# Adding gathered node rows to edge rows inside the indirect transfer of a graph network's edge stage

## The chip, the cores and the metric

The kernel is one program on 1 core of one Trainium2 chip. The metric is the device time of one launch in microseconds (us). Three runs of the kernel before gave 6792.09, 6813.02 and 6817.62 us; the median, 6813.02 us, is "the time before".

## The reference, cut to what matters

The network has four layers on 6250 nodes with 256 features each: a graph convolution, a routed feed-forward layer, a message-passing layer over 106250 edges, and a second routed feed-forward layer. The change touches only the third one. All arithmetic is in float32.

```python
def mish(x):
    return x * jnp.tanh(jax.nn.softplus(x))
x = mish(node_features @ W_dense.T + b_dense)      # one row of 256 per node
y = mish(edge_features @ W_edge.T + b_edge)        # one row of 256 per edge
msg = jax.nn.relu(x[src] + y)                      # gather a node row for each edge, add, relu
agg = jax.ops.segment_sum(msg, dst, num_segments=node_features.shape[0])
rst = x + agg
return mish(rst @ W_out.T + b_out)
```

The edges are sorted by their destination `dst`; the sources `src` are random.

## The kernel before

The program is a row of stages with a barrier of all engines between them. Two of them matter here.

**The node stage, `stage_node_mish`.** It makes x for all nodes, 52 tiles of 128 nodes in 13 groups of 4, each group as two halves h. For a half, TensorE (PE) transposes the normalised rows (`ps_t`), ScalarE (ACT) evacuates them, PE multiplies with the dense weights into `ps_y`, VectorE (DVE) clips the product into `q`, ACT makes a factor out of `q` with four activations, and DVE's `finish` turns factor and product into the mish rows: L1259 forms 1 - q, L1261 multiplies it by `ps_y` into `rows`. Only after L1261 is `ps_y[h]` free (`py_free`) for PE's next product. SyncE (SP) stores `rows` to the DRAM table `node_table`, from which the edge stage gathers; PE transposes `rows` back into `ps_u`, and DVE's `keep` (L1269) copies that into the feature table in SBUF (`c.feat`, "messages_table" in the profile), where the sums over edges are added later.

**The edge stage, `stage_edges`.** An earlier stage has left the mish of every edge row in the DRAM table `edge_mish_table`, with the sign turned: it holds -y. The edge stage has 210 groups of 512 edges (4 columns of 128 edges each, one edge per partition), walked as 35 iterations i of 6 slots s. The steps for one group are:

- SP loads the 512 KB of -y into one of three buffers `neg` (L1397), when `neg_free` says that the buffer's last group is summed.
- GpSimd (POOL) issues 4 indirect transfers (L1410), one for each column of 128 edges, which fetch the node rows `x[src]` into one of six buffers `node`. The row numbers come from `idx`, which DVE fills for three slots at once (`indices`, L1457). POOL waits for them once per three slots; nothing else holds it.
- DVE makes the 0/1 matrices `hot` (which edge belongs to which of 64 destinations, L1441), waits for `neg` and for the 4 gathers, and subtracts: `node - neg` (L1446), which is x + y.
- ACT applies relu in place (L1435).
- PE sums by 16 matmuls of `node` with `hot` into `ps_a` (L1425).
- DVE adds `ps_a` to the feature table (`add`, L1454).

DVE's queue goes: hot and subtraction for slot s, then the `add` of slot s-1, with the `indices` of the second half behind the `add` of step 0 and those of the next iteration's first half behind the `add` of step 3. So the index copy that lets POOL begin three slots stands behind a subtraction, and that subtraction waits for a gather. Every queue is in order, and the order is the written one.

## Time and profile before

| | us |
|---|---|
| median of three runs (lowest, highest) | 6813.02 (6792.09, 6817.62) |
| span of the profiled execution | 6977.8 |
| node stage, about 4300 to 4495 in the span | 195 |
| edge stage, about 4495 to 5880 in the span | 1385 |

The profiled execution is one run with the hardware profiler on. The profile gives its span, from the first to the last instruction, and no further time around it; the span is 164.8 us above the median. In the whole span PE is busy for 59% of the time, POOL 42%, DVE 29% and ACT 22%. POOL's time is nearly all the issue of indirect transfers.

### The profile page before, as it was taken

To read this page: it belongs to the slowest core of one execution; us is meant where nothing else is said; L and a number is where in the kernel's file an instruction comes from. 1 tells how busy PE (TensorE), PEld (TensorE's weight loads), DVE (VectorE), ACT (ScalarE), POOL (GpSimd) and SP (SyncE) were. 2 spreads that over 40 slices of the span, in tenths; PEclk is the share of its full clock that TensorE was granted. 3 is DMA by queue.
4 is the path that set the end of the run, shared out by engine and by line. 5 is a ranking of instruction groups with operands and counts; after the bars stand their busy time and mean duration, and the time that the engine had idled before them with its cause. 6 is when DMAs were issued, how large, how long until landed. Compare 5 with 4: busy or idle time off the path is not lost. (4 is left out here: it accounts for less than half of the span.)

```text
span 6977.8 us, 63984 instructions
## 1 busy us (share of the span) xinstructions
PE 4133.3 (59%) x16404; PEld 3120.9 (45%) x16404; DVE 2046.0 (29%) x4123; ACT 1510.4 (22%) x1776; POOL 2925.0 (42%) x3015
## 2 busy tenths in 40 slices
PE   3676666676567666666532962655555555616990
PEld 2444444444344444434322851455555554415780
DVE  4223222222222222222441334332222323421212
ACT  1223222223223222222210101311111112301110
POOL 0555554453455554454114013166666664041005
PEclk8666666666666666666566985655555555558995
DMA  2344443343233333233203222254554553013213
GB/s 93 119 130 134 131 132 124 120 135 115 94 104 112 102 102 104 95 98 103 52 23 111 82 84 60 68 162 155 161 162 159 160 165 101 1 60 116 66 59 112
DMA packets 347713, 744.50 MB, mean 107 GB/s; under 512 B 68177, under 2 KB 196313, under 8 KB 347538
## 3 DMA queue, kind: packets, MB, share of 16 engines
q1 hardware_dynamic: 161522, 392.68, 16.4%
q0 software_dynamic: 118176, 284.72, 14.2%
q10 hardware_dynamic: 67968, 66.60, 3.0%
q14 instruction: 33, 0.27, 0.0%
q8 instruction: 14, 0.23, 0.0%
HBM read 521.40 MB, written 222.32 MB: 107 GB/s over the span
## 5 line engine op out<-in xcount | busy, mean ns | idle before, releaser
L565 PE MATMUL conv_pz<-conv_we,conv_edge 128*128 128x256 f32 x3360 | 1394.5, 536 | 505.5 <-issue 500.4
L446 POOL DMA_INDIRECT conv_gath<-support_table,conv_idx x840 | 811.8, 966 | 890.0 <-POOLq L55 631.2
L1410 POOL DMA_INDIRECT x_node<-node_table,x_idx x840 | 874.0, 1040 | 711.5 <-POOLq L55 460.1
L446 POOL DMA_INDIRECT conv_gath<-hidden_table,conv_idx x840 | 807.2, 961 | 868.3 <-POOLq L55 619.5
L565 PEld LDWEIGHTS conv_pz<-conv_we,conv_edge 128*128 128x128 f32 x3360 | 794.9, 258 | 795.9 <-issue 677.2
L1425 PE MATMUL x_pa<-x_hot,x_node 128*128 128x64 f32 x3360 | 755.4, 422 | 627.5 <-PEq L55 377.0
L1425 PEld LDWEIGHTS x_pa<-x_hot,x_node 128*128 128x128 f32 x3360 | 729.1, 331 | 654.1 <-issue 654.1
L556 PE MATMUL conv_ps<-conv_hot,conv_gath 128*128 128x64 f32 x3360 | 588.2, 331 | 497.4 <-issue 200.6
L556 PEld LDWEIGHTS conv_ps<-conv_hot,conv_gath 128*128 128x128 f32 x3360 | 538.3, 243 | 537.8 <-issue 412.1
L1206 ACT ACTIVATE conv_q<-conv_q 128x1024 f32<-128x1024 f32 x210 | 221.9, 1057 | 2218.0 <-ACTq L55 1919.6
L456 DVE TENSOR_SCALAR conv_q<-conv_pz 128x1024 f32<-128x1024 f32 x210 | 257.2, 1225 | 1463.2 <-DVEq L55 1214.2
L1435 ACT ACTIVATE x_node<-x_node 128x1024 f32<-128x1024 f32 x210 | 221.8, 1056 | 1160.4 <-ACTq L55 1011.4
L1007 POOL COPY cb_idx<-row 128x8 int32 x24 | 4.8, 200 | 846.0 <-POOLq L55 845.9
L1110 PE MATMUL e_ph<-e_xt,e_w_first 128*128 128x256 f32 x1376 | 318.9, 389 | 61.9 <-PEq L55 61.9
L566 PE MATMUL conv_pz<-conv_bias_parts,conv_ones 3*128 3x256 bf16 x840 | 273.4, 326 | 100.7 <-issue 99.3
L1145 ACT ACTIVATE e_hid<-e_ph,e_b_first 128x256 f32<-128x256 f32 x344 | 138.1, 474 | 856.7 <-ACTq L55 856.7
L472 DVE TENSOR_TENSOR sums_table<-sums_table,conv_ps 128x64 f32 x420 | 93.2, 222 | 772.4 <-DVEq L55 614.7
L1110 PEld LDWEIGHTS e_ph<-e_xt,e_w_first 128*128 128x128 f32 x1376 | 262.7, 194 | 108.6 <-issue 73.3
L566 PEld LDWEIGHTS conv_pz<-conv_bias_parts,conv_ones 3*128 3x128 bf16 x840 | 78.9, 94 | 500.2 <-issue 500.2
L1446 DVE TENSOR_TENSOR x_node<-x_node,x_neg 128x1024 f32<-128x1024 f32 x210 | 257.0, 1224 | 149.8 <-DMA x_node<-node_table,x_idx 129.9
L1454 DVE TENSOR_TENSOR messages_table<-messages_table,x_pa 128x128 f32 x210 | 60.1, 286 | 769.8 <-DVEq L55 632.2
L272 PE MATMUL e_pt<-ident_sb,e_rows 128*128 128x128 f32 x456 | 61.4, 278 | 354.0 <-PEq L55 354.0
(213 smaller groups left out, 4461.1 us busy)
## 6 DMA issues: line engine op xcount, KB each, us to landing
conv_edge<-in_edge_t SPq DMA_DIRECT2D x210, 512.0 KB
edge_mish_table<-conv_neg SPq DMA_DIRECT2D x210, 512.0 KB
x_neg<-edge_mish_table SPq DMA_DIRECT2D x210, 512.0 KB
e_rows<-expert_rows SPq DMA_DIRECT2D x114, 256.0 KB, 3.7
expert_outs<-e_outs ACTq DMA_DIRECT2D x114, 256.0 KB, 2.2
expert_rows<-conv_zeros ACTq DMA_DIRECT2D x35, 512.0 KB
expert_outs<-conv_zeros ACTq DMA_DIRECT2D x35, 512.0 KB
conv_gath<-support_table,conv_idx POOLq DMA_INDIRECT x840
```

The source lines that it names most:

```text
L446: pool.indirect_dma_start(gath[s][:, j, :], None, table[:, :], bass.IndirectOffsetOnAxis(ap=idx[:, half, col:col + 1], axis=0),).then_inc( ...
L456: nc.vector.tensor_scalar(q[r][:], ps_z[r][:], ZMAX, None, ALU.min).then_inc(z_ready[r], 1)
L556: last = pe.matmul(ps[s % 2][:], gath[s][:, j, :], hot[half][:, at + j, :], start=j == 0, stop=j == CG - 1)
L565: pe.matmul(ps_z[r][:, j, :], edge[r][:, m, j * P:(j + 1) * P], we[:, m, :], start=m == 0, stop=False)
L566: last = pe.matmul(ps_z[r][:, j, :], ones[:], parts[:], start=False, stop=True)
L1110: last = pe.matmul(out[:, m, :], w[:, k, m * P:(m + 1) * P], given[:, k, :], start=k == 0, stop=k == KD - 1)
L1145: last = act.activation(hid[h][:, m, :], ps_h[h][:, m, :], (ACT.Relu, ACT.Gelu)[mix], bias=b_first[:, e, m:m + 1])
L1206: link(act, act.activation(q, q, ACT.Exp), own)
L1410: pool.indirect_dma_start(node[s][:, j, :], None, c.t3[:, :], bass.IndirectOffsetOnAxis(ap=idx[:, half, col:col + 1], axis=0),).then_inc(g ...
L1425: last = pe.matmul(ps_a[n][:, m, :], node[s][:, j, m * P:(m + 1) * P], hot[n][:, j, :], start=j == 0, stop=j == CG - 1)
L1435: act.activation(node[s][:], node[s][:], ACT.Relu).then_inc(msg_ready, 1)
L1446: nc.vector.tensor_tensor(node[s][:], node[s][:], neg[s % RING][:], ALU.subtract).then_inc(own, 1)
```

## The change

It has three parts.

- The edge stage no longer has `neg` buffers. SP loads the -y rows into `node[s]` itself, six buffers instead of three, and the indirect transfers add the gathered rows onto them (`compute_op=ALU.add`). POOL therefore waits for SP's load (`neg_in[s]`) before the 4 transfers of every slot. SP waits for `node_free[s]`, which DVE signals when the slot's sum is ready.
- The subtraction L1446 is gone. ACT waits for the gathers itself and applies relu with scale -1. DVE's matrices get a semaphore of their own (`hot_ready`), for which PE waits beside `msg_ready`.
- For this, the gathered rows have to be -x. The node stage makes them in one instruction, (q - 1) * `ps_y`, in place of the two of `finish`; `keep` turns the sign back with a multiplication in place of the copy.

```diff
             def finish(h):
                 take(dve, q_ready[h])
-                link(dve, nc.vector.tensor_scalar(q[h][:], q[h][:], -1.0, 1.0, ALU.mult, ALU.add), own)
                 take(dve, rows_out[h], 16)
-                link(dve, nc.vector.tensor_tensor(rows[h][:], q[h][:], ps_y[h][:], ALU.mult), own)
+                link(dve, nc.vector.scalar_tensor_tensor(rows[h][:], q[h][:], -1.0, ps_y[h][:], ALU.add, ALU.mult), own)
...
-                nc.vector.tensor_copy(tokens(c.feat[:, :, :], g, h), ps_u[h][:])
+                nc.vector.tensor_scalar(tokens(c.feat[:, :, :], g, h), ps_u[h][:], -1.0, None, ALU.mult)
...
                     for s in range(SLOTS):
-                        take(sp, neg_free[s % RING])
-                        sp.dma_start(neg[s % RING][:], c.mish_d[...]).then_inc(neg_in[s % RING], 16)
+                        take(sp, node_free[s])
+                        sp.dma_start(node[s][:], c.mish_d[...]).then_inc(neg_in[s], 16)
...
                         take(pool, idx_ready[half])
                         for s in range(half * 3, half * 3 + 3):
+                            take(pool, neg_in[s], 16)
                             for j in range(CG):
                                 col = (s - half * 3) * CG + j
                                 pool.indirect_dma_start(
                                     node[s][:, j, :], None, c.t3[:, :],
                                     bass.IndirectOffsetOnAxis(ap=idx[:, half, col:col + 1], axis=0),
+                                    compute_op=ALU.add,
                                 ).then_inc(gathered[s], 16)
...
+                        take(pe, hot_ready)
                         take(pe, msg_ready)
...
-                        take(act, own)
-                        act.activation(node[s][:], node[s][:], ACT.Relu).then_inc(msg_ready, 1)
+                        act.wait_ge(gathered[s], k * (IT * CG * 16) + i * (CG * 16) + CG * 16)
+                        act.activation(node[s][:], node[s][:], ACT.Relu, scale=-1.0).then_inc(msg_ready, 1)
...
-                take(dve, neg_in[s % RING], 16)
-                dve.wait_ge(gathered[s], k * (IT * CG * 16) + i * (CG * 16) + CG * 16)
-                nc.vector.tensor_tensor(node[s][:], node[s][:], neg[s % RING][:], ALU.subtract).then_inc(own, 1)
...
                 take(dve, sum_ready)
-                dve.sem_inc(neg_free[s % RING], 1)
+                dve.sem_inc(node_free[s], 1)
```

DVE's queue at the start of the edge stage's steady loop, before, for slot 0 and half of slot 1 (x_hot are the 0/1 matrices, x_node the gathered rows, x_idx the row numbers for POOL):

```order
L1441 TENSOR_TENSOR x_hot<-iota_sb,x_rel 128x256
L1445 ISA
L1446 TENSOR_TENSOR x_node<-x_node,x_neg 128x1024
L1449 ISA
L1449 TENSOR_LOAD x_window
L1449 ISA x2
L1454 ISA
L1454 TENSOR_TENSOR messages_table<-messages_table,x_pa 128x2x64
L1457 ISA
L1457 COPY x_idx<-src_sb 128x12
```

The same place with the change:

```order
L1443 TENSOR_TENSOR x_hot<-iota_sb,x_rel 128x256
L1448 ISA
L1448 TENSOR_LOAD x_window
L1448 ISA x2
L1453 ISA
L1453 TENSOR_TENSOR messages_table<-messages_table,x_pa 128x2x64
L1456 ISA
L1456 COPY x_idx<-src_sb 128x12
```

The subtraction has left the queue. What stands behind it, the addition of the slot before and the index copy, now stands behind the 0/1 matrices alone.

POOL's loop over one iteration, before (a row names the semaphores for which the first of its transfers waits; the names are those of earlier stages that held the same semaphores, here the two `idx_ready`):

```order
L1410 DMA x_node<-node_table,x_idx 128x256 [waits s_rows_ready0]
L1410 DMA x_node<-node_table,x_idx 128x256 x11
L1410 DMA x_node<-node_table,x_idx 128x256 [waits s_rows_out1]
L1410 DMA x_node<-node_table,x_idx 128x256 x11
```

With the change, for the first half and the first slot of the second:

```order
L1410 DMA x_node<-node_table,x_idx 128x256 [waits s_py_ready1,s_rows_out1]
L1410 DMA x_node<-node_table,x_idx 128x256 x3
L1410 DMA x_node<-node_table,x_idx 128x256 [waits conv0_w_in]
L1410 DMA x_node<-node_table,x_idx 128x256 x3
L1410 DMA x_node<-node_table,x_idx 128x256 [waits conv0_edge_in1]
L1410 DMA x_node<-node_table,x_idx 128x256 x3
L1410 DMA x_node<-node_table,x_idx 128x256 [waits s_rows_ready0,conv0_edge_in2]
L1410 DMA x_node<-node_table,x_idx 128x256 x3
```

The 12 transfers of a half are cut into three times 4, each behind a wait for the slot's load; the wait for the indices has stayed where it was.

## Rows read from the trace of the kernel before

**Rows 1.** Windows of node and edge stage: busy us of each engine, clock, DMA share, GB/s.

```profile
4300.00:4495.00 195.00, 153.65 (x468) 91.41 (x468) 78.54 (x154) 80.73 (x131) 0.00 (x0) 0.64 0.10 35
4495.00:5880.00 1385.00, 755.41 (x3360) 729.06 (x3360) 403.26 (x706) 221.84 (x210) 874.71 (x841) 0.50 0.51 159
```

**Rows 2.** Groups by line, 4520 to 5860: busy us, mean ns, idle before, releasers.

```profile
L1410 POOL DMA_INDIRECT x_node<-node_table,x_idx x822 | 855.5, 1041 | 486.2 <-issue 245.9 <-POOLq L55 240.0 <-DVE x_idx L1457 0.3
L1425 PE MATMUL x_pa<-x_hot,x_node 128*128 128x64 f32 x3279 | 737.2, 422 | 603.3 <-PEq L55 354.3 <-issue 220.4 <-ACT x_node L1435 28.3
...
L1446 DVE TENSOR_TENSOR x_node<-x_node,x_neg 128x1024 f32<-128x1024 f32 x205 | 250.9, 1224 | 129.7 <-DMA x_node<-node_table,x_idx 109.8 <-issue 9.6 <-DVEq L55 9.3
```

**Rows 3.** Waits, 4520 to 5860: total us, times, longest.

```profile
POOL x_node L1410 <- POOLq L55: 240.0, 34, 13.1
DVE x_node L1446 <- DMA x_node<-node_table,x_idx: 109.8, 49, 4.8
```

**Rows 4.** The tile x_node: duration min, median, max in ns.

```profile
L1410 POOL DMA_INDIRECT x_node<-node_table,x_idx x840: 942/949/2002, 4498.1 to 5862.5; - x168
```

**Rows 5.** Timeline of the edge stage, three stretches: start us, length us, what.

```profile
5212.87 1.22 DVE L1446 TENSOR_TENSOR x_node<-x_node,x_neg 128x1024 f32<-128x1024 f32 x1
...
5214.08 0.95 POOL L1410 DMA_INDIRECT x_node<-node_table,x_idx  x1 [0.30 <-issue]
5214.21 1.06 ACT L1435 ACTIVATE x_node<-x_node 128x1024 f32<-128x1024 f32 x1 [3.95 <-ACTq L55]
...
5215.41 3.65 PE L1425 MATMUL x_pa<-x_hot,x_node 128*128 128x64 f32 x16 [1.36 <-issue]
...
5228.22 0.29 DVE L1454 TENSOR_TENSOR messages_table<-messages_table,x_pa 128x128 f32 x1 [14.13 <-issue]
...
5255.54 0.17 DVE L1457 COPY x_idx<-src_sb 128x12 int32 x1 [0.24 <-DVEq L55]
...
5256.52 1.52 POOL L1410 DMA_INDIRECT x_node<-node_table,x_idx  x1 [3.33 <-POOLq L55]
...
5258.28 1.22 DVE L1446 TENSOR_TENSOR x_node<-x_node,x_neg 128x1024 f32<-128x1024 f32 x1 [0.20 <-DVEq L55]
5258.35 1.98 POOL L1410 DMA_INDIRECT x_node<-node_table,x_idx  x1 [0.30 <-issue]
...
5267.09 0.96 POOL L1410 DMA_INDIRECT x_node<-node_table,x_idx  x1 [0.30 <-issue]
...
5267.72 0.43 DVE L1441 TENSOR_TENSOR x_hot<-iota_sb,x_rel 128x256 f32<-128x256 f32 x1
```

**Rows 6.** Other indirect transfers of the span: busy us, mean ns.

```profile
L446 POOL DMA_INDIRECT conv_gath<-support_table,conv_idx x840 | 811.8, 966 | 890.0 <-POOLq L55 631.2 <-issue 258.7
...
L955 POOL DMA_INDIRECT expert_rows<-sc_xn,sc_idx x196 | 193.6, 988 | 73.6 <-issue 57.7 <-POOLq L55 10.0 <-POOL sc_idx L964 4.9
```

**Rows 7.** DMA queues, 4520 to 5860: packets, MB, share of 16 engines.

```profile
q0 software_dynamic: 39343, 107.51, 26.9%
q1 hardware_dynamic: 29376, 106.97, 23.6%
```

**Rows 8.** Other DMA by line, whole span: KB each, us to landing.

```profile
e_w_first<-in_m_w POOLq DMA_DIRECT2D x8, 512.0 KB, 8.6
e_rows<-expert_rows SPq DMA_DIRECT2D x114, 256.0 KB, 3.7
```

**Rows 9.** Timeline of one half of the node stage.

```profile
4388.95 0.42 DVE L1259 TENSOR_SCALAR n_q<-n_q 128x512 f32<-128x512 f32 x1
...
4389.18 1.08 PE L272 MATMUL n_pt<-ident_sb,n_xn 128*128 128x128 f32 x4 [0.60 <-PEq L55]
...
4389.63 0.69 DVE L1261 TENSOR_TENSOR n_rows<-n_q,n_py 128x512 f32<-128x512 f32 x1 [0.26 <-DVEq L55]
...
4390.61 2.04 PE L1342 MATMUL n_py<-n_wd,n_xt 128*128 128x256 f32 x4 [0.35 <-PEq L55]
```

**Rows 10.** Waits of the node stage, 4306 to 4492: total us, times, longest.

```profile
PE n_py L1342 <- PEq L55: 14.3, 24, 1.8
```

More of the change, by code:

```diff
@@ L1371, in stage_edges @@
         window = sb("window", [1, EG], I32)
-        neg = [sb(f"neg{n}", [P, CG, D]) for n in range(RING)]
         node = [sb(f"node{s}", [P, CG, D]) for s in range(SLOTS)]
@@ L1375, in stage_edges @@
         ps_a = [pb(f"pa{n}", [P, KD, W]) for n in range(RING)]
-        own, add_own = sem("own"), sem("add_own")
+        add_own = sem("add_own")
         idx_ready = [sem(f"idx_ready{half}") for half in range(2)]
-        neg_in = [sem(f"neg_in{n}") for n in range(RING)]
-        neg_free = [sem(f"neg_free{n}") for n in range(RING)]
-        msg_ready, sum_ready = sem("msg_ready"), sem("sum_ready")
+        neg_in = [sem(f"neg_in{s}") for s in range(SLOTS)]
+        node_free = [sem(f"node_free{s}") for s in range(SLOTS)]
+        msg_ready, hot_ready, sum_ready = sem("msg_ready"), sem("hot_ready"), sem("sum_ready")
         gathered = [nc.alloc_semaphore(f"x_gathered{s}") for s in range(SLOTS)]
@@ L1389, in _ @@
         def _(sp):
-            for n in range(RING):
-                sp.sem_inc(neg_free[n], 1)
+            for s in range(SLOTS):
+                sp.sem_inc(node_free[s], 1)
             with sp.Fori(0, load_passes(sp)) as k:
@@ L1394, in _ @@
                     for s in range(SLOTS):
-                        take(sp, neg_free[s % RING])
-                        sp.dma_start(neg[s % RING][:], c.mish_d[bass.ds(i * SLOTS + s, 1)].rearrange("a p j d -> p (a j) d")
-                                     ).then_inc(neg_in[s % RING], 16)
+                        take(sp, node_free[s])
+                        sp.dma_start(node[s][:], c.mish_d[bass.ds(i * SLOTS + s, 1)].rearrange("a p j d -> p (a j) d")
+                                     ).then_inc(neg_in[s], 16)
         @block.gpsimd
@@ L1433, in _, with one_hots @@
                     for s in range(SLOTS):
-                        take(act, own)
-                        act.activation(node[s][:], node[s][:], ACT.Relu).then_inc(msg_ready, 1)
+                        act.wait_ge(gathered[s], k * (IT * CG * 16) + i * (CG * 16) + CG * 16)
+                        act.activation(node[s][:], node[s][:], ACT.Relu, scale=-1.0).then_inc(msg_ready, 1)
         @block.vector
         def _(dve):
-            def message(k, i, s):
+            def one_hots(i, s):
                 nc.vector.tensor_tensor(hot[s % RING][:], c.iota[:].unsqueeze(1).to_broadcast([P, CG, W]),
                                         rel[:, bass.ds(i * (SLOTS * CG) + s * CG, CG)].unsqueeze(2).to_broadcast([P, CG, W]),
-                                        ALU.is_equal)
-                take(dve, neg_in[s % RING], 16)
-                dve.wait_ge(gathered[s], k * (IT * CG * 16) + i * (CG * 16) + CG * 16)
-                nc.vector.tensor_tensor(node[s][:], node[s][:], neg[s % RING][:], ALU.subtract).then_inc(own, 1)
+                                        ALU.is_equal).then_inc(hot_ready, 1)
             def add(i, s):
@@ L1461, in step @@
                 for s in range(SLOTS):
-                    message(k, i, s)
+                    one_hots(i, s)
                     add(i if s else i - 1, (s - 1) % SLOTS)
@@ L1474, in _ @@
                 for s in range(SLOTS):
-                    message(k, 0, s)
+                    one_hots(0, s)
                     if s:
```

## The prediction

> **What bounds the kernel now.** I first read the windows of the two stages that the change touches. The node stage is 195 us with PE busy for 153.65 of them; the edge stage is 1385 us, 6.6 us for each of its 210 groups, and there no engine is full: POOL 874.71 us, PE 755.41 (at the lower of the two clock levels, 0.50), DVE 403.26, ACT 221.84, and the DMA engines have a share of 0.51 [rows 1].
>
> Then the groups by line, for who waits for whom. POOL is the nearest to a bound. Each gather takes 1041 ns on average and about 0.30 us pass before the next one (245.9 us for 822) [rows 2], so a group costs 4 x 1.34 = 5.4 us of POOL. The rest is the 240.0 us in 34 waits that POOL spends for its indices [rows 3]. 855.5 + 245.9 + 240.0 = 1341 us is the whole window of 1340 us: POOL is either issuing or waiting for its indices.
>
> Why are indices late? The timeline shows it: POOL issues every 1.25 us without a break, ACT and PE have finished a group at 5215.41 + 3.65 = 5219.06, and DVE's addition of the group before, whose matmuls were still earlier in PE's queue, starts only at 5228.22 after 14.13 us of idleness [rows 5]. DVE waits there for PE's signal, and the profile doesn't say what delays that signal. The change doesn't touch it. The index copy stands behind this addition, and POOL resumes right behind the copy (copy at 5255.54, gather at 5256.52) [rows 5].
>
> **The edge stage: what goes.** (a) Some gathers are long: the median is 949 ns, the longest 2002 [rows 4]. The long ones stand beside the subtraction: 1.98 us for the gather that starts 0.07 us after an L1446, while one beside L1441 takes 0.96 [rows 5]. In total, 840 x (1.041 - 0.949) = 77 us. With L1446 gone I expect all gathers near the median, so -77 us, and as POOL is never free otherwise this is on the path. It can't be more than 77, and if the length has another cause it is 0.
>
> The Trainium skill has a rule for this (SBUF — State Buffer, practical consequences of the shared port): a VectorE instruction with two SBUF inputs contends with a GpSimd instruction that reads SBUF. L1446 has two such inputs and the gather reads its indices; the trace agrees [rows 5]. L1441 has two as well and lengthens nothing there, so the rule alone would give a little less than 77 back.
>
> (b) The path from a gather's landing to the index copy loses the subtraction, 1.22 us (1224 ns [rows 2]) and its hand-over of 0.12 (the relu at 5214.21 follows a subtraction that began at 5212.87 [rows 5]). Where POOL waits for indices, it waits 1.34 us less: 34 x 1.34 = 46 us. Besides, the addition no longer stands behind a DVE wait for the next slot's gather (109.8 us in all [rows 3]); a third of the additions stand ahead of an index copy, so up to 37 us more. I take 46 and keep 0 and 83 as ends.
>
> (c) DVE's other savings, 257 us of busy time less the above, are worth nothing: DVE is 29% busy in the stage and waits. ACT's relu keeps its 1.06 us [rows 5] with a scale. PE's second wait costs nothing, as DVE makes the matrices ahead.
>
> **The edge stage: what comes.** (d) The transfer that adds. No row shows one. On POOL: indirect gathers of 512 B rows take 966 ns, scatters of 1 KB rows 988 [rows 6], gathers of 1 KB rows 949; neither size nor direction matters much. An adding transfer must fetch the destination too, which could be one more list of addresses. From below it costs 0 more; from above, a second transfer's whole issue, +0.95 us on each of 840, +797 us. I take the nearest row, the scatter: 988 - 949 = 39 ns, 840 x 0.039 = +33 us.
>
> (e) On the DMA engines: the gathers hold 26.9% and the loads 23.6% of the 16 engines in a window with 6.56 us per group [rows 7], so 1.76 and 1.55 us per group. From below the adding gather costs the same 1.76; from above, with the old row read in and the sum written as well, it is three times that, 5.3 us, and with the load 6.8 us per group. I take twice, 3.5 + 1.55 = 5.1 us, which lies just under POOL's 5.15 (4 x (0.988 + 0.30)): nothing on the path, but without reserve.
>
> A rule of the Trainium skill speaks against the change here (Collectives: The Full Stack, on why ReduceScatter is half of AllGather): an add in the DMA engine needs two source reads, and the measured ratio is 1.93. By it the share of the gathers would be 26.9% x 1.93 = 52%, and 5.0 us per group with the load, an estimate from that page; no run here shows it yet. The sum would be unchanged, since POOL still needs a little more.
>
> (f) The new wait of POOL for the slot's load. Behind the waiting instruction stand all later gathers. The load starts when the slot's last group is summed. A 256 KB load lands in 3.7 us, a 512 KB one behind others in 8.6 [rows 8]. POOL comes back to a slot 25 us after it left it (five slots of 5 us), and in an undisturbed run the slot is summed after landing (DVE's 49 waits for one average 2.2 us [rows 3]), relu 1.06, matmuls 3.65 and addition 0.29 [rows 5], with the hand-overs some 8 us; 8 + 8.6 = 17, so 8 us of cover. Where the sums come late and together, the cover is gone, and a load of some 3.7 us shows (rival C). I take 0, and 126 as the dear end.
>
> **The node stage.** L1259 (0.42 us) and its link go: L1261 starts 0.68 us later than L1259 [rows 9], and so the bank is free 0.68 us earlier. PE's product L1342 waits for it 0.35 us behind its transposes [rows 9], 14.3 us in 24 waits in all [rows 10]. What is late next is PE's own transposes, which end at 4390.26, so a step gains 0.35 and not 0.68: 24 x 0.35 = -8 us, with ends 0 and -14. The sign turned in `keep` costs the same copy out of the bank.
>
> **Sum.** -77 - 46 + 33 - 8 = -98 us. On the profiled span of 6977.8 us that gives 6880. The span is 165 us above the median of 6813.02; nothing says in which stage that lies, so I carry the difference over whole: 6813 - 98 = 6715 us.
>
> **The rivals.** Half a per cent, 34 us, is about what a measurement of this kernel can tell from no change.
>
> A, the adding transfer costs POOL clearly more, as a list of addresses more per row. For: POOL is the bound, 840 issues in a row, so 0.1 us more on each is 84 us; break-even is at (77 + 46 + 8) / 840 = 0.16 us above 949 ns. Against: size and direction made no difference so far [rows 6]. At a third to a half more than 949 ns (0.32 to 0.47): 6813 - 131 + 269 to 395 = 6950 to 7080 us; middle 7010.
>
> B, the DMA engines become the bound. For: at twice the cost there is no reserve left, and loads and gathers come in bursts. Against: the share now is 0.51 [rows 1]. At three times, 6.8 us per group: 210 x (6.8 - 6.56) = +50 on the profiled stage and more for the landings that each slot now waits for in a row (load, then gather); 6860 to 7000 us.
>
> C, the load is exposed: POOL's wait for indices is replaced by one for the load behind it, in the 34 places where sums come late. It costs 34 x 3.7 = 126 us and eats the gain: 6715 + 126 = 6840 us, at the edge of no change. For: the load now can't run ahead of the sum by another buffer. Against: the sum of slot 0 is usually over long before the one that releases the indices.
>
> D, nothing moves: the stage is paced by the late signals from PE, and what POOL gains it waits for. 6805 us. For: idle times of 14 us. Against: POOL has no other idle time than those 240 us.
>
> **Chances.** Forecast 0.48; A 0.20; B 0.14; C 0.11; D 0.07. Forecast, faster by over 0.5%: 0.48. Within 0.5%: nearly all of C and D, 0.16. Slower: A and B with the rest, 0.36. The likeliest case alone reaches from 6640 (ends of a, b, node stage, d at 0: 6813 - 77 - 83 - 14) to 6770. A and B stretch the range to 7020, which leaves out the dear half of A and little below.
>
> **What would show it.** (a) The line of L1410 has a mean within 20 ns of its median. (d) Its median says the price directly: under 1.0 us the forecast holds, over 1.11 it fails. (e) The share of the software queue q0 in the stage: about 50% for twice. (b, f) POOL's waits behind L55 in the stage: under 240 us if the path got shorter, over it if loads are exposed; in C they are of about 4 us and follow a load's issue. The node stage is 187 us long instead of 195. A stage of about 1280 us in the profile makes the forecast right; one of 1385 or more with POOL's instruction unchanged would say that the landings, not the issue, pace it, and would make my reading of the bound wrong.

## The result: 3.1% slower

The changed kernel takes 7015.93 us (median of 4 runs, 6982.77 to 7056.43). The kernel before takes 6805.92 us beside it (6792.09 to 6817.62). The ratio is 1.031, with an interval of 1.027 to 1.035: 210 us slower, where I forecast 98 us faster. The profiled execution of the changed kernel took 7003.71 us, with a span of 7001.9.

The two stages went opposite ways. Windows of the changed kernel (length, then busy us of PE, PE's weight loads, DVE, ACT, POOL, then clock, DMA share, GB/s), node stage first:

```profile
4196.00:4331.00 135.00, 100.68 (x450) 62.78 (x450) 66.61 (x126) 79.25 (x128) 0.00 (x0) 0.93 0.14 51
4338.00:5903.00 1565.00, 765.94 (x3360) 732.60 (x3360) 159.60 (x487) 221.80 (x210) 1299.17 (x840) 0.50 0.70 140
```

The edge stage grew from 1378 to 1564 us, from the first transfer's start to the last addition's (before 4498.1 to 5876.2, after 4338.6 to 5902.5). The node stage shrank from 195 to 143 us, from its first normalisation (L263) to its last copy into the feature table (before 4299.1 to 4493.8, after 4188.3 to 4331.4), and its clock rose from 0.64 [rows 1] to 0.91 over all of it, 0.93 in the window above. These two stages give +186 and -52 us. What stands ahead of them, which the change doesn't touch, took 111 us less in the changed kernel's profiled execution, so that the two spans differ by only 24 us where the medians differ by 210: the profile of the kernel before is one 165 us above its median, and the profiles don't say where the rest of the 210 us lies. The pair e15 and e16 below settles the price better.

Groups by line, changed kernel, 4520 to 5860 (busy us, mean ns, idle before and releasers):

```profile
L1410 POOL DMA_INDIRECT x_node<-node_table,x_idx x724 | 1119.7, 1547 | 220.5 <-issue 201.9 <-POOLq L55 18.6
L1427 PE MATMUL x_pa<-x_hot,x_node 128*128 128x64 f32 x2897 | 660.6, 423 | 680.0 <-PEq L55 680.0
L1437 ACT ACTIVATE x_node<-x_node 128x1024 f32<-128x1024 f32 x181 | 191.2, 1056 | 1149.0 <-DMA x_node<-node_table,x_idx 1149.0
L1453 DVE TENSOR_TENSOR messages_table<-messages_table,x_pa 128x128 f32 x181 | 52.3, 289 | 1145.7 <-DVEq L55 1145.7
```

1119.7 + 201.9 + 18.6 = 1340.2 us: POOL fills the window of 1340 us. Its waits, by the view of waits of the same stretch, are nowhere longer than the gap that stands between any two transfers (total us, times, longest):

```profile
POOL x_node L1410 <- issue: 201.9, 663, 0.3
POOL x_node L1410 <- POOLq L55: 18.6, 61, 0.3
```

So the 240.0 us in 34 waits [rows 3] are gone entirely, and the stage is still longer, because one transfer now occupies POOL for 1547 ns instead of 1041 [rows 2]. The tile view (min/median/max ns) and the DMA queues of 4520 to 5860 (packets, MB, share of 16 engines) of the changed kernel:

```profile
L1410 POOL DMA_INDIRECT x_node<-node_table,x_idx x840: 1537/1546/1623, 4338.6 to 5891.8; - x168
```

```profile
q0 software_dynamic: 104212, 94.91, 50.5%
q1 hardware_dynamic: 26060, 94.90, 20.3%
```

The timeline of one group of the changed kernel shows the rhythm: four transfers at 1.85 us, then relu, matmuls and addition with no delay between them:

```profile
5000.83 3.65 PE L1427 MATMUL x_pa<-x_hot,x_node 128*128 128x64 f32 x16 [3.71 <-PEq L55]
5001.38 1.55 POOL L1410 DMA_INDIRECT x_node<-node_table,x_idx  x1 [0.30 <-issue]
5003.23 1.55 POOL L1410 DMA_INDIRECT x_node<-node_table,x_idx  x1 [0.30 <-issue]
5004.80 0.29 DVE L1453 TENSOR_TENSOR messages_table<-messages_table,x_pa 128x128 f32 x1 [6.40 <-DVEq L55]
5005.08 1.55 POOL L1410 DMA_INDIRECT x_node<-node_table,x_idx  x1 [0.30 <-issue]
```

PE ends at 5004.48 and DVE adds at 5004.80. In the kernel before, an addition came after 14.13 us of idleness although PE had long finished [rows 5]. I count a sum as *held* when DVE gets past its wait for PE's signal over 0.5 us after PE's last matmul of that group has ended and DVE has nothing left to do before that wait (an index copy apart). Over the 210 groups of each trace: before 79 held sums, 606 us in all, the longest 21.1 us; after none. Where exactly a wait is taken to begin shifts such a count by a few sums and its total by up to 3%.

The trace of before excludes three simple explanations. The other signals of the chain aren't held: in all 210 groups relu begins at most 0.13 us after the subtraction has ended and ACT is free, and PE's matmuls at most 0.15 us after relu has ended and PE is free, also while POOL issues its transfers. DVE isn't busy or stuck in an earlier instruction: in the stretch of rows 5 its queue has reached the wait at 5213.38, and gets past it at 5227.93. And it isn't the loading of code: the DMA records hold only 2 instruction packets in the whole edge stage.

The bill of the edge stage: the adding transfer +840 x (1.547 - 0.949) = +502 us; no more lengthening by the subtraction -77; POOL's idle time between its first and last transfer, 491 us before and 256 after, -236 (37 waits, 247 us with the usual 0.30 of each, have shrunk to 0.30). That makes +189, and with 4 us less at the end +186 us.

### The profile page after: what moved, and what is told of

It is laid out like the page before. It is cut to its first block and busy times, and to the rows that moved or that the text cites. A ratio compares the mean times of both kernels' runs of the same rounds, so it can differ in the third digit from the quotient of the medians.

```text
span 7001.9 us, 63723 instructions
## 1 busy us (share of the span) xinstructions
PE 4096.4 (59%) x16404; PEld 3105.8 (44%) x16404; DVE 1796.3 (26%) x3887; ACT 1510.3 (22%) x1776; POOL 3374.5 (48%) x3015
## 5 line engine op out<-in xcount | busy, mean ns | idle before, releaser
L1410 POOL DMA_INDIRECT x_node<-node_table,x_idx x840 | 1299.2, 1547 | 427.1 <-issue 233.3
L463 DVE SCALAR_TENSOR_TENSOR conv_neg<-conv_q,conv_pz 128x1024 f32<-128x1024 f32 x210 | 254.7, 1213 | 7.9 <-DVEq L55 7.9
```

The costliest lines, as they stand in the source:

```text
L463: link(dve, nc.vector.scalar_tensor_tensor(neg[r][:], q[r][:], -1.0, ps_z[r][:], ALU.add, ALU.mult), neg_own)
L1410: pool.indirect_dma_start(node[s][:, j, :], None, c.t3[:, :], bass.IndirectOffsetOnAxis(ap=idx[:, half, col:col + 1], axis=0), compute_op= ...
```

## The experiments

Two questions were open. Is the price of the adding transfer really its own, and not one of load, landing or DMA traffic? And where did the held sums go? The runs were made on five chips. Times are compared only with the kernel before on the same chip. Lengths of stages come from one profiled execution each and are also set beside those of other chips: that of the edge stage with adding transfers is 1563.9, 1562.2 (e3) and 1563.1 us (e15) in three traces. "Held" is the number of held sums, their total and the longest. "Stage" is the edge stage in the profile, and T the time between the starts of two transfers in a row (median).

**e1, the node stage's part alone.** The edge stage keeps its subtraction, now an addition of -y and -x with the sign turned in relu.

```diff
-                nc.vector.tensor_tensor(node[s][:], node[s][:], neg[s % RING][:], ALU.subtract)
+                nc.vector.tensor_tensor(node[s][:], node[s][:], neg[s % RING][:], ALU.add)
-                        act.activation(node[s][:], node[s][:], ACT.Relu)
+                        act.activation(node[s][:], node[s][:], ACT.Relu, scale=-1.0)
```

> The kernel before with the node stage's part of the change alone: the rows are made with the turned sign by one VectorE instruction, and the edge stage adds neg instead of subtracting it, with relu at scale -1. Everything else in the edge stage is as before. In the changed kernel's profile the node stage took 135 us instead of 189, with the TensorE clock granted at 0.93 instead of 0.64. Theory 1 (the shorter loop is what lets the clock rise, so it belongs to the change): the node stage is 130 to 140 us long at a clock above 0.85, and the kernel takes about 6806 - 53 = 6753 us. Theory 2 (the edit gives only the 8 us of my sum, and the clock came from somewhere else): about 6798 us, node stage 180 to 187 us long.

Measured: 6878.64 against 6905.22 us, ratio 0.993 (0.989 to 0.998). Node stage 139 us at a clock of 0.95, edge stage 1388.9, held 72, 581 us, 21.0. The node stage's part gives its gain alone (the whole moved by 27 us, where theory 1 expected 53, at an interval of 14 to 79), and nothing of it reaches the edge stage.

**e2, the changed kernel whose transfer doesn't add.**

```diff
-                                    compute_op=ALU.add,
```

> The changed kernel with one thing taken out: the indirect transfers of the edge stage overwrite the loaded rows instead of adding to them, so the edge part of each message is left out. All waits, loads and orders stay. Theory 1 (the price is POOL's issue of an adding transfer, 1.55 us against 0.95): L1410 falls to a median of about 0.95 us, a group to 5.0 us, the edge stage to about 1060 us from 1564, the kernel to about 6520 us. Theory 2 (POOL's new wait for the load, or the longer row of load and gather for each buffer, paces the stage too): the stage stays above 1250 us and the kernel above 6700 us. Theory 3 (VectorE's subtraction is what lengthened some gathers before): the mean of L1410 is within 20 ns of its median here, where no subtraction runs.

Measured: 6923.84 against 6905.22, ratio 1.003 (0.998 to 1.008). The tile view of e2:

```profile
L1410 POOL DMA_INDIRECT x_node<-node_table,x_idx x840: 943/949/1088, 4339.5 to 5738.8; - x168
```

The price is the operation's own: 949 ns without it, 1546 with it, all else equal. The maximum of 1088 ns, without any subtraction, also confirms that L1446 made gathers long (up to 2002 [rows 4]). The trace of before says it directly: the 297 transfers during which an L1446 ran took 77.4 us more than 949 ns each would, the other 543 together nothing; beside L1441 alone none took over 1142 ns. But the stage is 1411.6 us and not 840 x 1.254 = 1053: the held sums are back, 79, 798 us, 21.2. The numbers are those of theory 2, but POOL's waits for the loads follow the late sums, for which the loads wait in turn. The timeline of e2:

```profile
4739.68 9.17 PE L1426 MATMUL x_pa<-x_hot,x_node 128*128 128x64 f32 x42
...
4751.75 0.29 DVE L1452 TENSOR_TENSOR messages_table<-messages_table,x_pa 128x128 f32 x1 [8.08 <-DVEq L55]
...
4753.24 3.65 PE L1426 MATMUL x_pa<-x_hot,x_node 128*128 128x64 f32 x16 [4.39 <-DVE x_hot L1442]
4753.35 0.95 POOL L1410 DMA_INDIRECT x_node<-node_table,x_idx  x1 [1.33 <-issue]
...
4767.12 0.94 POOL L1410 DMA_INDIRECT x_node<-node_table,x_idx  x1 [0.30 <-issue]
...
4771.55 0.29 DVE L1452 TENSOR_TENSOR messages_table<-messages_table,x_pa 128x128 f32 x1 [18.61 <-DVEq L55]
...
4773.11 0.29 DVE L1452 TENSOR_TENSOR messages_table<-messages_table,x_pa 128x128 f32 x1 [0.61 <-DVEq L55]
```

PE finished one group at 4748.85 and the next at 4756.89. DVE gets to add the first only at 4771.5, some 3.5 us after POOL's row of 12 transfers has ended (4768.06). The profile models the ends of matmuls, but that PE began the next group at 4753.24 shows that it wasn't still at work on the first.

**e3, the changed kernel with a quarter of the load.**

```diff
-                        sp.dma_start(node[s][:], c.mish_d[...])
+                        sp.dma_start(node[s][:, 0:1, :], c.mish_d[...])
```

> The changed kernel with a quarter of the load: SyncE loads only the first of the four 128-edge columns of a group (128 KB instead of 512 KB), the other three columns keep what was there (buffers are zeroed once at the start), so three quarters of the edge parts are left out. The adding transfers are unchanged. Theory 1 (POOL's issue sets the pace): no change against the changed kernel, 7016 us within 20, edge stage 7.4 us a group. Rival (the DMA engines are the bound, 50.5% of them for the gathers and 20.3% for the loads): the loads' share falls to about 5%, and the stage with it by a fifth, to about 1250 us, the kernel to about 6700 us.

Measured: 7051.02 against 6905.22, ratio 1.017 (1.001 to 1.032); stage 1562.2 beside the 1563.9 of the changed kernel, held 0. In the queues of e3, 4600 to 5700, the load has shrunk and the gathers' share hasn't:

```profile
q0 software_dynamic: 85655, 78.01, 51.6%
q1 hardware_dynamic: 21456, 19.54, 5.5%
```

15 points less traffic change nothing: neither the DMA engines (rival B) nor the load (C) set the stage.

**e4, e1 with a gate for each slot.** POOL waits for `node_free[s]` before each slot, and DVE copies the indices before the addition.

```diff
                         for s in range(half * 3, half * 3 + 3):
+                            take(pool, node_free[s])
...
                     message(k, i, s)
+                    if s % 3 == 2 and not final:
+                        indices(i + 1, s // 3)
                     add(i if s else i - 1, (s - 1) % SLOTS)
```

> The kernel of the first experiment (plain gathers, VectorE adds) with finer gates for POOL: the index copy of a half is made three steps earlier, behind the wait that shows that the half's gathers were issued, and POOL waits for each slot's sum (node_free) before it gathers into that slot, instead of for three slots' sums at once. Theory 1 (POOL's 240 us of waits for indices are on the path, and a gate per slot takes away most): the waits fall under 100 us, the edge stage to 1120 to 1200 us, the kernel 80 to 150 us under the first experiment, so 6610 to 6670 us. Rival (the stage is paced by the late sums themselves, and POOL only waits elsewhere): within 20 us of the first experiment.

Measured: 6830.5 against 6905.22, ratio 0.986 (0.974 to 0.997); stage 1301.0, held 95, 590 us, 20.1. POOL reaches further before it must wait, but the sums are held as before, and the stage misses the 1120 to 1200 us of theory 1.

**e5 and e6, a break after every transfer.** e5 is e2 with a memset of 500 columns and a wait for it after each gather, e6 is e1 with one of 64 columns.

```diff
                                 ).then_inc(gathered[s], 16)
+                                link(pool, nc.gpsimd.memset(pad[:], 0.0), pad_own)
```

> The kernel of the second experiment (plain transfers, the edge part of each message left out), with a GpSimd memset of 500 columns and its semaphore between the transfers, so that POOL issues one about every 1.9 us as in the changed kernel, instead of every 1.25. In the second experiment the stage took 1412 us with 110 sums signalled over 1 us late (1476 us together), in the changed kernel 1564 us and none late. Theory 1 (PE's signals are late when transfers are issued at the full rate; the adding transfer only spaces them out): hardly any late sum, a stage of 210 x 4 x 1.9 = about 1600 us, POOL without a wait. Theory 2 (late signals belong to plain transfers, whatever their rate): late sums stay, and with them waits of POOL, the stage over 1650 us.

> The kernel of the first experiment (node stage's part alone, VectorE adds) with a small GpSimd memset (64 columns) and its semaphore between the transfers of the edge stage, about 0.3 us each, so one transfer about every 1.55 us. Theory 1 (late signals come from the full issue rate and go with wider spacing): late sums mostly gone, a stage of about 6.3 us a group, 1310 to 1330 us instead of 1389, the kernel 50 to 80 us under the first experiment's. Theory 2 (late signals stay): the stage is longer than the first experiment's, 1440 us or more, as the memsets come on top.

Measured: e5 (two runs) 7502.81 against 6854.38, ratio 1.099 (1.083 to 1.116), T 2.29 us, stage 1999.1, held 0. e6 7092.89, ratio 1.036 (1.022 to 1.050), T 1.93 us, stage 1669.0, held 0. So it isn't the adding that frees the sums: plain gathers with something between them do it too. Both stages missed their expected lengths, because a break opens 0.98 us and more and not the 0.3 that I had counted on.

**e7, e2 with rows of half the bytes.**

```diff
-                                    node[s][:, j, :], None, c.t3[:, :],
+                                    node[s][:, j, 0:HID], None, c.t2[:, :],
```

> The kernel of the second experiment with the plain transfers fetching 128 columns (512 B rows of another table) instead of 256, so half of the gathered data is left out; POOL's issue is the same 0.95 us. Theory 1 (the issue rate delays PE's signals): late sums and the stage stay as they were, 1476 us late and 1412 us long, within a tenth. Theory 2 (the moved bytes delay them): late sums fall to half or less and the stage to under 1250 us.

Measured: 6871.46 against 6854.38, ratio 1.005 (1.000 to 1.011); median transfer 944 ns, stage 1427.9, held 71, 810 us, 22.0. Half the bytes hold sums just as much, so traffic isn't the cause. The software queue of e2 and of e7, 4700 to 5700 (597 and 584 transfers):

```profile
q0 software_dynamic: 28699, 78.40, 27.2%
q0 software_dynamic: 18660, 38.27, 15.3%
```

A transfer of e7 has 32 packets instead of 48, and takes POOL 944 ns instead of 949.

**e8, only the first of four transfers adds.**

```diff
-                                    compute_op=ALU.add,
+                                    **({"compute_op": ALU.add} if j == 0 else {}),
```

> The changed kernel with only the first of the four transfers of a group adding, the other three plain (so three quarters of the edge parts are left out). POOL's issue is then 1.55 + 3 x 0.95 and four gaps of 0.30, 5.6 us a group. If the price of the change were the issue of adding transfers alone, the stage would be 1180 us. By theory 1 (late signals return as the mean spacing falls to 1.40 us) it stays at 1300 to 1420 us, with late sums between the none of the changed kernel and the 1476 us of the second experiment.

Measured (two runs): 6712.77 against 6854.38, ratio 0.983 (0.970 to 0.997); mean transfer 1.122 us, stage 1241.7, held 95, 416 us, 8.2. One slow transfer in four shortens the holding and costs little.

**e9, the kernel before with one break after every 4 gathers of the edge stage; e12, with one per 12, after the second of three slots.**

```diff
                                 ).then_inc(gathered[s], 16)
+                            link(pool, nc.gpsimd.memset(pad[:], 0.0), pad_own)
```

> The kernel before with one edit: after the four transfers of a group POOL makes a small memset and waits for its semaphore, a break of about 0.67 us once per group. Theory 1 (PE's signals are held back while POOL issues plain transfers one behind the other, and pass in a break): the longest late sum falls from 21 us to under 10, as it did where one transfer in four was an adding one (8.2 us), and the stage from 1378 to about 1270 to 1320 us although POOL has 140 us more to do; the kernel 60 to 100 us faster than before. Theory 2 (what helped there was something else about the adding transfer): the late sums stay at 20 us and the stage is 1400 us or longer, the kernel the same as before or slower.

> The kernel before with the break only once per half, after the second of its three groups, so runs of 8 and 4 transfers instead of 12. Theory 1: the longest late sum lies between the 21 us of runs of 12 and the under 10 us of runs of 4, at 12 to 16 us, the stage between the two as well. Theory 2: 20 us as before.

Measured: e9 6914.45 against 6930.37, ratio 0.996 (0.992 to 1.001), stage 1359.2, held 0. e12 (two runs) 6833.18, ratio 0.984 (0.976 to 0.991), stage 1290.0, held 112, 469 us, 14.3. The timeline of e9:

```profile
5005.12 0.95 POOL L1412 DMA_INDIRECT x_node<-node_table,x_idx  x1 [0.30 <-issue]
5006.07 0.17 POOL L1416 MEMSET x_pad<- 128x64 f32 x1
5007.05 0.95 POOL L1412 DMA_INDIRECT x_node<-node_table,x_idx  x1 [0.81 <-issue]
```

A break opens 0.98 us instead of 0.30 between two transfers. Longer unbroken rows of transfers go with longer holding. The rows are longer than the program's order suggests, since POOL mostly finds its indices ready: in the trace of before, of 39 rows 11 have 12 transfers, 25 have 24 and 3 have 36, and the longest holding beside them is 18.8, 21.1 and 19.4 us. In e12 no row is over 12 (43 rows of 12, 27 of 8, 27 of 4), and the longest is 14.3; in e9 none is over 4, and nothing is held. A fixed dose isn't shown (beside rows of 12 the longest is 7.5 us in e14 and 18 in e13), and the end of a row isn't needed: 45 of the 79 holdings of before end while the row goes on. An adding transfer in every four (e8, 8.2 us) is a weaker remedy than a break. In e9 the 210 breaks cost nearly what they bring: 0.68 us each, and the gathers meet the subtraction more often (394 of them instead of 297), which lengthens them by 125 us instead of 77. So the stage missed the 1270 to 1320 us expected.

**e10, e4 with e9's break; e11, with the same break in the two convolution stages as well**, whose POOL loop is built alike and which the change doesn't touch. Its diff is that of e9 at L447.

> The kernel of the fourth experiment (node stage's part, plain transfers, VectorE adds, a gate per slot) with the same break once per group. It took 0.986 of the time before and its stage 1301 us, with 590 us of late sums. Theory 1: late sums under 10 us each, the stage near POOL's floor of 4 x 1.34 + 0.67 = 6.0 us a group, 1265 us, and the kernel about 0.98 of the time before. Theory 2: the break only adds its 140 us, stage 1400 us, kernel slower than the fourth experiment's.

> As the kernel before this one in the list, with the same break also in the two convolution stages after every four transfers. There POOL has slack (it is busy for about half of those stages), and VectorE takes PE's product up to 24 us after PE's last matmul. Theory 1 (the same hold-up of PE's signals costs time there): the two stages, 3250 us together, get 100 us or more shorter. Theory 2 (PE is the bound there, and the late take is VectorE's own order): no change, within 20 us.

Measured: e10 6906.12 (6754.43 to 6976.92, ten runs) against 6930.37, too scattered for a ratio; stage 1360.3 where 1265 was expected, held 0. e11 **6313.17** us, ratio **0.908** (0.902 to 0.913), stage 1359.7, held 0. The convolution stages have the kernel's largest loss. Windows of the kernel before and of e11 over these stages:

```profile
150.00:3380.00 3230.00, 2114.55 (x7524) 1384.45 (x7525) 876.02 (x1287) 904.96 (x852) 1618.98 (x1680) 0.66 0.36 113
```

```profile
150.00:2800.00 2650.00, 2011.45 (x7583) 1354.80 (x7583) 886.19 (x1296) 913.51 (x860) 1689.75 (x2100) 0.73 0.45 139
```

The same work in 580 us less, though POOL does more. The traces show that it is the same holding: of the 630 waits of DVE for PE in these two stages (sums and products), before holds 109, for 1213 us in all, the longest 22.4 us, and e11 159, for 596 us, the longest 9.6 us. So here a break after every 4 transfers shortens the holding to half and doesn't end it.

**e13, the gates of e4, breaks of e11 in the convolution stages, the rare one of e12 in the edge stage.**

> Plain gathers in the edge stage with a gate for each slot, the node stage's part of the change, the break (memset of 64 columns and its semaphore) after every 4 gathers in both convolution stages, and in the edge stage only after every third slot's 4 gathers. Theory 'POOL's unbroken row of transfers holds PE's signals': the convolution stages keep their gain of some 600 us, and the edge stage, with runs of at most 12 transfers that are cut once, is between e4_slot_gates (1301 us) and e12_rare_break (1290): some 1240 to 1290 us, and the whole 6220 to 6310 us. Rival 'gates and breaks do the same thing and don't add': the edge stage stays at 1290 to 1300 and the whole at 6250 to 6310; a stage of 1360 or more would say that breaks cost their gap whatever else is done.

Measured: **6228.51** against 6937.03, ratio **0.897** (0.890 to 0.903), the best of this study: 10% below the kernel before on the same chip, and so below the changed one too. Stage 1288.3, held 91, 534 us, 18.0. Gates and rare breaks don't add up (e4 1301, e12 1290), as the rival said; the last gather of the convolution stages ends at 2765 us, in e11 at 2799.

**e14, e11 with a bare semaphore trip as its break.**

```diff
-                            link(pool, nc.gpsimd.memset(pad[:], 0.0), pad_own)
+                            pool.sem_inc(pad_own, 1)
+                            take(pool, pad_own)
```

> As e11_all_breaks, but each break is only POOL raising a semaphore and waiting for it, with no memset. Theory 'any semaphore trip of POOL releases PE's signals': no addition in the edge stage waits over 0.5 us beyond PE's last matmul, the stage is shorter than e11's 1360 us because the gap is shorter (a gap of 0.3 to 0.6 us instead of 1.1 gives 1250 to 1310 us), the convolution stages keep their gain, and the whole is 6150 to 6300 us. Rival 'it needs the longer gap or an instruction that POOL executes': late sums of up to 21 us are back, the stages before the node stage end near 3250 to 3370 us, and the whole is 6750 to 6880 us.

Measured: 6771.6 against 6937.03, ratio 0.976 (0.968 to 0.983). Stage 1290.5, held 86, 567 us, 19.6; convolution stages until 3287, with 125 held and 1122 us. Timeline of e14 across a slot's end, where the trip has vanished in the usual gap:

```profile
4702.97 0.94 POOL L1418 DMA_INDIRECT x_node<-node_table,x_idx  x1 [0.30 <-issue]
4704.21 0.94 POOL L1418 DMA_INDIRECT x_node<-node_table,x_idx  x1 [0.30 <-issue]
4705.46 0.95 POOL L1418 DMA_INDIRECT x_node<-node_table,x_idx  x1 [0.31 <-issue]
4706.71 0.95 POOL L1418 DMA_INDIRECT x_node<-node_table,x_idx  x1 [0.30 <-issue]
```

A wait of POOL alone doesn't free the sums.

**e15 and e16, both kernels with the break in the convolution stages alone.**

> The changed kernel with the break (memset and semaphore) after every 4 gathers in both convolution stages alone. The edge stage keeps its adding transfers of 1.55 us and stays at 1564 us. Theory 'the hold-up in the convolution stages is the same thing and independent of the change': those stages end near 2800 us in the span instead of 3270, the whole is 7016 less 450 to 600, that is 6420 to 6560 us, 80 to 210 us above e16_before_conv. Rival 'the gain in the convolution stages came with the edge stage's breaks, as through the clock or memory traffic': under 200 us gained.

> The kernel before with the same break in both convolution stages alone, the edge stage untouched. Theory: convolution stages end near 2800 us instead of 3377, edge stage 1378 us with late sums of up to 21 us as before, the whole some 6240 to 6400 us. The difference to e15_after_conv is then the price of the change alone: edge stage +186, node stage -53, so +130 us; as in the first comparison +210 us would say that stages outside the two that were changed shift as well. Rival (the edge stage's breaks matter for the rest): over 6600 us.

Measured, against 6937.03: e15 (changed) 6496.05 (6488.67 to 6503.49), ratio 0.935 (0.928 to 0.942), stage 1563.1, held 0. e16 (before) 6385.19 (6376.0 to 6399.89), ratio 0.919 (0.912 to 0.926), stage 1386.2, held 81, 614 us, 21.0. With over half of the convolution stages' holding gone (545 us left in e16, 369 in e15), the change costs 111 us, where I expected 130: edge stage +177, node stage -40 (183 to 143), -31 ahead of them in stages that it doesn't touch, the rest outside. The node stage of e16, with nothing changed in it but a clock of 0.73 instead of 0.64, is 11 us shorter than that of before:

```profile
3717.00:3900.00 183.00, 135.89 (x463) 80.39 (x461) 78.12 (x152) 80.21 (x130) 0.00 (x0) 0.73 0.11 37
```

**e17, e11 without waiting for the memset; e18, e11 with 12 semaphore trips instead of memset and wait.** They were to tell whether an instruction or a gap frees the sums.

```diff
-                            link(pool, nc.gpsimd.memset(pad[:], 0.0), pad_own)
+                            take(pool, pad_own)
+                            nc.gpsimd.memset(pad[:], 0.0).then_inc(pad_own, 1)
```

> As e11_all_breaks, but POOL doesn't wait for the memset's end before the next transfer (it waits for it only before the next memset, when it is long done). Theory 'an instruction that POOL executes between the transfers is what releases PE's signals': no late sums in the edge stage, a stage under 1340 us, conv stages that end near 2800 us, the whole 6150 to 6310 us. Rival 'it is POOL's wait or the gap': late sums of up to 18 to 21 us, conv stages that end near 3290 us, the whole 6750 to 6830 us.

> As e11_all_breaks, with 12 bare semaphore trips of POOL in place of the memset and its one trip: a gap without an instruction that POOL executes. If a trip takes some 0.06 us or more, the gap is 0.7 us or longer. Theory 'time without a transfer being issued is what releases PE's signals': late sums 0 or under 1 us, and the whole 6250 to 6400 us. Rival 'it takes an executed instruction': late sums as in e14 (86 of them, up to 20 us) and the whole 6750 to 6950 us. If the trips vanish in the 0.30 us again, it tells nothing.

Measured: e17 5716.52, ratio 0.996 (0.992 to 1.000), stage 1161.9, held 0; e18 (two runs) 5641.48, ratio 0.983 (0.980 to 0.986), stage 1102.1, held 0. All expectations missed, because on this chip the kernel *before* took only 5738.56 us, where it took 6806 to 6937 on the others. The timeline of e18 has 12 trips of a semaphore before the transfer at 4006.52, and no gap for them:

```profile
4005.18 1.04 POOL L1419 DMA_INDIRECT x_node<-node_table,x_idx  x1 [0.30 <-POOLq L55]
4006.52 0.94 POOL L1419 DMA_INDIRECT x_node<-node_table,x_idx  x1 [0.30 <-POOLq L1424]
```

POOL issues as densely as in e14, and yet no sum is held. So on this chip dense issue doesn't hold sums, and breaks there are worth nothing or little. The convolution stages agree: not one of their 630 waits is held in e17 or e18, and in e18 their last gather ends at 2374 us, where in before it ends at 3378 and in e11, with its breaks, at 2799. The question of e17 and e18 is open: there was nothing to free.

## Why the prediction was wrong

The forecast was 98 us faster, and the kernel is 210 us slower. That 7015.93 us lies just inside the range of 6640 to 7020 is no merit of the forecast: rivals A and B had stretched the range that far.

- **The bound** (POOL issues or waits for indices; no engine or DMA queue is full): right. It stayed the bound, and e3 shows that traffic isn't one.
- **(a) -77 us** for gathers no longer lengthened: right. Without L1446 mean and median agree (1547 and 1546 ns; in e2 the maximum is 1088), and the 297 transfers beside it held all 77 us of the excess. The Trainium skill's rule on VectorE with two SBUF inputs and GpSimd (SBUF — State Buffer, practical consequences of the shared port) agrees in direction.
- **(b) -46 us, ends 0 and -83**: the term was too small. All 247 us of waits went. They were set not by the 1.34 us of path that I cut but by held sums, and these vanished with the rhythm. I had seen the 14.13 us of idleness [rows 5] and wrote "the change doesn't touch it". It did: e5, e6 and e9 show that the spacing of POOL's transfers decides it, e2 and e7 that neither the adding nor the bytes do.
- **(c) 0** for DVE's and ACT's savings: right. DVE's busy time fell from 403.26 us [rows 1] to 159.60, and bought nothing beside (a) and (b).
- **(d) +33 us for the adding transfer: this is the step that failed.** I took "the nearest row, the scatter", 39 ns above the gather. Measured: +597 ns per transfer, +502 us. It lies within the ends that I kept (0 to +797), so the error was to go by the row that resembled it most. No row of the trace showed a transfer that has to fetch its destination, so none was near. The packets differ: 104212 / 724 = 144 per adding transfer against 39343 / 822 = 48 before [rows 7]. By the sizes in the DMA records the same 128 KB go in 128 packets of 1 KB instead of 32 of 4 KB, each time with 16 small ones of 4 B. That the packets are what POOL's time goes into isn't shown and doesn't fit e7, whose transfers have a third fewer packets and cost POOL only 5 ns less. What POOL does in the 597 ns is open.
- **(e) DMA engines at twice the cost, not on the path**: right. 50.5% of 1340 us over 181 groups is 3.74 us per group, 2.1 times the 1.76 of before. With the load it is 5.2 us of 7.4. The 1.93 for two source reads that the Trainium skill gives (Collectives: The Full Stack, on why ReduceScatter is half of AllGather) for a collective's addition is near the 2.1 measured here.
- **(f) 0 for the wait for the load**: right, no wait above 0.3 us.
- **The node stage, -8 us**: the direction right, the term too small: -52 in the profiles, -40 between e16 and e15. Four lines of the timeline of the changed kernel (start, length):

```profile
4255.26 0.69 DVE L1272 TENSOR_SCALAR n_q<-n_py 128x512 f32<-128x512 f32 x1 [1.69 <-DVEq L55]
...
4256.51 0.68 DVE L1260 SCALAR_TENSOR_TENSOR n_rows<-n_q,n_py 128x512 f32<-128x512 f32 x1
...
4257.48 1.10 PE L1341 MATMUL n_py<-n_wd,n_xt 128*128 128x256 f32 x4
...
4260.23 0.69 DVE L1272 TENSOR_SCALAR n_q<-n_py 128x512 f32<-128x512 f32 x1 [1.70 <-DVEq L55]
```

  A half takes 4.97 us (4255.26 to 4260.23). The granted clock was 0.93, near the level of 2.4 GHz, where before it was 0.64, between the two levels; 4 matmuls of the dense product took 2.04 us [rows 9] and now 1.10. The instruction removed is worth at most 0.68 us on each of 26 halves, 18 us; the rest goes with the clock: PE's busy time in the stage fell from 154 to 107 us for the same 468 matmuls. The edit of this stage raises it, not the edge stage's: from the first normalisation to the last copy the clock was 0.91 to 0.97 in all 16 traces with the edit (137 to 143 us) and 0.60 to 0.74 in the four without it (183 to 198 us: before, e9, e12, e16). Why it rises is open.

Of the rivals, A had the mechanism (the adding transfer costs POOL clearly more) and by its sum nearly the time (7010 us). It was right by two errors: its price (0.32 to 0.47 us) was too low, its waits saved (46) too few. B and C are excluded by e3 and by the waits, D by the new rhythm.

What is shown: the transfer's price (after against e2), and that on the chips of e1 to e16 DVE learns late of PE's sums while POOL issues plain transfers every 1.25 us (e2 and e7 bring it back, e5, e6 and e9 take it away), but not on the chip of e17 and e18. What is open: by what mechanism, whether an instruction or a gap of POOL ends it, and why one chip was free of it. On that chip the change was not run. An estimate from e18's stage (1102 us, with gates, which the kernel before lacks) and the changed kernel's 1564 us: 460 - 50 = at most some 400 us or 7% slower there, since there would be no held sums to save.

## What to carry to other kernels

Before a transfer is made to add, price the instruction that issues it: here 128 rows of 1 KB cost POOL 1.55 us instead of 0.95, and where POOL's issue is the bound, nothing that DVE saves pays for it. When two engines' end and start lie many us apart with nothing between them, measure what that idle time follows before you call it untouched: here one cheap break (a memset of 64 columns and a wait) after every 4 indirect transfers was worth 8% in the stages nobody had meant to change. Compare only on one chip, and repeat on another: what gained 8 to 10% on two chips may be worth nothing on a third.

## What the runs showed of the hardware

- DVE learned of PE's finished sums up to 22 us late while POOL issued plain indirect transfers at 1.25 us each, in rows of 12 to 36; with 1.85 us each, or in the edge stage with a memset and wait per 4, never over 0.5 us late. In the convolution stages the same break left up to 10 us (e11, e15). In the trace of before, signals from DVE to ACT and from ACT to PE came within 0.15 us all the while.
- A semaphore trip of POOL, and even 12 of them, fits into the 0.30 us between two transfers.
- The kernel before ran in 5738.56 us on one chip, and in 6806 to 6937 us on the others. In the two traces from that chip (e17, e18) no wait of DVE for PE is held, in any of the three stages with gathers.
- An indirect transfer that adds 128 rows of 1 KB took POOL 1546 ns, a plain one 949 (e2) and one of 512 B rows 944 (e7); a plain one beside a subtraction of 1.22 us up to 2002.
- With one DVE instruction of 0.42 us per half gone, the node stage's granted clock was 0.91 to 0.97 in 16 traces, instead of 0.60 to 0.74 in four; why is open.
